# Layer 0's attention: values and row sums stored by DMA into turned tiles, and divided at the end

## The reference

```
h = layernorm(x) * (1 + ca) + sa
q, k, v = h @ W_query[n], h @ W_key[n], h @ W_val[n]        # per head n, width 8
att = softmax(q @ k.T * 8 ** -0.5)                          # 2048 x 2048 per head
x = x + ga * sum over n of (att @ v) @ W_out[n]
```

## Time and profile before

| what | us |
|---|---|
| median of 3 executions | 1732.26 |
| lowest and highest | 1729.99 and 1733.25 |
| span of the profiled execution | 1727.5 |
| VectorE busy in the span | 1303.3 (75%) |
| TensorE busy in the span | 1241.6 (72%) |
| ScalarE busy in the span | 890.0 (52%) |

### The profile page before, as it was taken

The page is one execution under the profiler, slowest core; times in us unless marked ns, Lnnn a source line. Parts: engine busy times, 40 slices in busy tenths (PEclk is TensorE's granted clock), DMA queues, the critical chain, the costliest instruction groups (busy, mean ns, idle before and its releaser), DMA issues. The chain is left out here.

```text
span 1727.5 us, 29793 instructions
## 1 busy us (share of the span) xinstructions
PE 1241.6 (72%) x10670; PEld 618.5 (36%) x10674; DVE 1303.3 (75%) x3511; ACT 890.0 (52%) x1757; POOL 235.6 (14%) x275
## 2 busy tenths in 40 slices
PE   7799999999999997575994463060315989823676
PEld 4122222222222223354983342040104556623445
DVE  5999999999999971447237336989898469668783
ACT  4099999999999997312421122020001675612463
POOL 2000000000000000003410314030001321100223
PEclk9599999999999999677995586575656898965668
DMA  2100000001000000000004331000001721022001
GB/s 69 41 10 27 25 20 21 21 26 27 27 21 20 21 3 1 15 30 1 1 1 183 102 86 47 0 0 1 1 1 26 208 70 47 18 101 63 22 22 31
DMA packets 45031, 62.88 MB, mean 36 GB/s; under 512 B 12785, under 2 KB 34357, under 8 KB 44485
## 3 DMA queue, kind: packets, MB, share of 16 engines
q1 hardware_dynamic: 38243, 49.71, 9.7%
q0 software_dynamic: 5440, 10.67, 2.5%
q10 hardware_dynamic: 1200, 0.59, 0.1%
HBM read 34.10 MB, written 13.63 MB: 28 GB/s over the span
## 5 line engine op out<-in xcount | busy, mean ns | idle before, releaser
L842 ACT ACTIVATE l0att_probs<-l0att_ps_sv 128x512 f32<-128x512 f32 x960 | 521.2, 596 | 79.7 <-PE l0att_ps_sv L811 67.9
L888 DVE TENSOR_REDUCE l0att_half_negmax<-l0att_ps_m 128x1 f32<-128x1024 f32 x480 | 547.0, 1215 | 5.3 <-PE l0att_ps_m L741 5.3
L773 PE MATMUL l0att_ps_sv<-l0att_probs,l_V_aug 128*32 128x256 f32 x4096 | 325.3, 392 | 4.8 <-ACT l0att_pv_sb L833 4.7
L811 PE MATMUL l0att_ps_sv<-l_Q,l_K 51*128 51x512 bf16 x992 | 194.4, 388 | 4.0 <-ACT l0att_probs L850 2.4
L741 PE MATMUL l0att_ps_m<-l_K,l_Q 48*128 48x512 bf16 x960 | 185.9, 384 | 11.1 <-DVE l0att_half_negmax L888 7.1
L773 PEld LDWEIGHTS l0att_ps_sv<-l0att_probs,l_V_aug 128*32 128x32 f32 x4096 | 83.0, 108 | 197.1 <-issue 100.5
L811 PEld LDWEIGHTS l0att_ps_sv<-l_Q,l_K 51*128 51x128 bf16 x992 | 48.0, 92 | 207.4 <-ACT l0att_probs L842 188.1
L472 POOL CAST l0att_nm<-l0att_negmax 128x16 bf16<-128x16 f32 x16 | 3.1, 196 | 514.5 <-DVE l0att_negmax L864 514.5
L2862 ACT ACTIVATE l3loc_probs<-l3loc_ps_s 128x320 f32<-128x320 f32 x128 | 48.9, 435 | 36.0 <-PE l3loc_ps_s L2839 35.4
L2040 DVE SCALAR_TENSOR_TENSOR l2spk_lif_v<-l2spk_U 128x64 f32<-128x64 f32 (+1 forms) x368 | 61.6, 211 | 0.0
L2305 PE MATMUL l2spk_ps<-l_X,l2spk_w_terms 128*128 128x512 bf16 x48 | 13.2, 445 | 62.3 <-DVE l_X L2335 62.3
(11 more groups left out here) (736 smaller groups left out, 2392.5 us busy)
## 6 DMA issues: line engine op xcount, KB each, us to landing
l_K<-l_kp SPq DMA_DIRECT2D x192, 32.0 KB
l_Q<-l_qp SPq DMA_DIRECT2D x192, 32.0 KB
l1ffn_W<-in_l_expert_w_dram SPq DMA_DIRECT2D x1, 4096.0 KB
l3f_experts_l_w<-in_l_w_dram SPq DMA_DIRECT2D x2, 2048.0 KB
l_sorted_in<-l1ffn_zeros SPq DMA_DIRECT2D x1, 3072.0 KB
l1exp_rows<-l_sorted_in SPq DMA_DIRECT2D x6, 512.0 KB, 5.6
l_sorted_out<-l1exp_y SPq DMA_DIRECT2D x6, 512.0 KB, 4.6
l_Q<-in_local_mask_q_dram POOLq DMA_DIRECT2D x2, 1170.0 KB, 18.8
```

The source lines that it names most:

```text
L773: mm = pe.matmul(ps_v[32 * c:32 * c + 32, cols], V_aug[:, kt, h, :], probs[:, kt % 2, c, cols], start=(kt == 0 and part == 0), stop=(kt == ...
L811: pe.matmul(dst, K[at, h % HEAD_BUFS, c1(kt)], Q[at, h % HEAD_BUFS, c4(2 * pair + i)], start=True, stop=True).then_inc(last_scored[i] if l ...
L842: act.activation(probs[:, kt % 2, c, :], ps_s[:, n % 3, :], ACT.Exp).then_inc(expd, 1)
L888: dve.tensor_reduce(half_negmax[:, h % 2, t, half:half + 1], src, AX_X, ALU.max, negate=True).then_inc(m_read, 1)
```

## The change

The turned form of the values is not left any more. `V_aug` gets 8 columns of ones instead of one, so `ps_v` holds the row sum 8 times, in rows 8 to 15 of each block. After ScalarE's copy, 8 transfers a head (4 blocks, values and sums) put the rows of `pv_sb` into `OT` and `den`, both [128, 2048] with head and value along the partitions. For heads 0 to 14 SP issues them; for head 15 SP, ScalarE and POOL share them. Heads 0 to 11 are divided in one piece on VectorE during the last head (`DIVIDED` = 96 rows), where the reciprocals of heads 12 to 14 are taken too. For head 15, the reciprocal is taken of the copied tile, and that is stored. The last 32 rows are multiplied in the output stage, one block of 512 tokens at a time. The turns of values on TensorE, the `"pv"` turns, the per-head reciprocal and multiplication, and the turning and copying of the output stage are gone. ScalarE's copy into a `pv_sb` buffer waits for the stores of the head two before it. `stage_project_out` stays for layer 3.

```diff
                 pool.wait_ge(norm.tile_normed, NT)
-                pool.memset(V_aug[:, :, :, L0_K + 1:], 0.0).then_inc(v_filled, 1)
-                pool.memset(V_aug[:, :, :, L0_K:L0_K + 1], 1.0).then_inc(v_filled, 1)
+                pool.memset(V_aug[:, :, :, L0_K + sums:], 0.0).then_inc(v_filled, 1)
+                pool.memset(V_aug[:, :, :, L0_K:L0_K + sums], 1.0).then_inc(v_filled, 1)
...
-def stage_l0_attend(nc, loads, g, V_aug, qp, kp, Q, K, ones_placed, loaded_first, O):
+STORES = 2 * NC4
+DIVIDED = 96
+def store_last(eng, OT, den, last_sb, copied, c, which, stored):
+    eng.wait_ge(copied[which], (L0_H, 1)[which])
+    store_rows(eng, OT, den, last_sb[which], L0_H - 1, c, which, stored)
+def store_rows(eng, OT, den, pv, h, c, which, stored):
+    rows = slice(L0_K * h, L0_K * (h + 1))
+    eng.dma_start((OT, den)[which][rows, c4(c)],
+                  pv[32 * c + L0_K * which:32 * c + L0_K * (which + 1), :]).then_inc(stored, 16)
+def stage_l0_attend(nc, loads, g, V_aug, qp, kp, Q, K, ones_placed, loaded_first, OT, den, heads_stored, last_stored):
...
         plan = {}
-        for s in range(-1, L0_H + 1):
-            slots = range(LEAD if s < 0 else NT if s < L0_H else 1)
+        for s in range(-1, L0_H):
+            slots = range(LEAD if s < 0 else NT)
...
                 uses = []
-                if s >= L0_H - 1 and kt == 3 * (L0_H - s):
-                    uses.append(("pv", s - 1))
...
                     place[what] = len(turns)
-                    if what[0] == "nm" and what[1] >= 2:
-                        place["pv", what[1] - 2] = len(turns)
...
             def _(sp):
+                def store_head(sp, h):
+                    sp.wait_ge(pv_copied, h + 1)
+                    for c in range(NC4):
+                        for which in range(2):
+                            store_rows(sp, OT, den, pv_sb[:, h % 2, :], h, c, which, heads_stored[h % 2])
...
                         load_piece(sp, Q, K, qp, kp, h, loaded[h % HEAD_BUFS], *piece)
+                    if h >= HEAD_BUFS:
+                        store_head(sp, h - HEAD_BUFS)
+                for h in range(L0_H - HEAD_BUFS, L0_H - 1):
+                    store_head(sp, h)
+                for c, which in ((0, 0), (0, 1), (3, 0)):
+                    store_last(sp, OT, den, last_sb, (pv_copied, rsum_done), c, which, last_stored[c])
...
                     splits_of(link, pool, [nm[:, h % 2, i, :] for i in range(3)], rest[:], negmax[:], nm_ready)
-                    if h >= 2:
-                        pool.wait_ge(nm_copied, h - 1)
-                    else:
-                        pool.wait_ge(m_read, place["nm", h] + 1)
+                    pool.wait_ge(m_read, place["nm", h] + 1)
...
                                        nm_rows[:, h % 2, :]).then_inc(nm_placed[h % 2], 16)
+                for which in range(2):
+                    store_last(pool, OT, den, last_sb, (pv_copied, rsum_done), 2, which, last_stored[2])
...
                             "p s t -> p (s t)"), ident16[:])
-                        if h >= 2:
-                            mm = turn_values(h - 2, dst)
-                    else:
-                        mm = turn_values(what[1], dst)
                     mm.then_inc(m_filled, 1)
-                def turn_values(h, dst):
-                    pe.wait_ge(pv_copied, h + 1)
-                    for i in range(4):
-                        mm = pe.transpose(dst[:, c1(i)], pv_sb[:, h % 2, c1(i)], g.ident[:])
-                    return mm
...
                     values(L0_H - 1, NT - 1, part)
-                run(("pv", L0_H - 1))
...
                     if h >= 2:
-                        act.wait_ge(m_filled, filled_by[place["pv", h - 2]])
+                        act.wait_ge(heads_stored[h % 2], 16 * STORES * (h // 2))
...
                 copy_values(L0_H - 1)
+                for c, which in ((1, 0), (1, 1), (3, 1)):
+                    store_last(act, OT, den, last_sb, (pv_copied, rsum_done), c, which, last_stored[c])
...
                                       ALU.min).then_inc(negmax_ready, 1)
-                def normalise(h, src):
-                    v = src[:, 0:BANK].rearrange("p (i c k) -> p i c k", i=4, c=NC4)
-                    if h >= 1:
-                        dve.wait_ge(m_read, place["pv", h - 1] + 1)
-                    link(dve.reciprocal(rden[:], v[:, :, :, L0_K]))
-                    o = O[:, :, L0_K * h:L0_K * (h + 1)].rearrange("p (c i) k -> p i c k", c=NC4)
-                    dve.tensor_tensor(o, v[:, :, :, 0:L0_K], bcast(rden[:].unsqueeze(3), P, 4, NC4, L0_K),
-                                      ALU.mult).then_inc(m_read, 1)
...
                         dve.tensor_copy(nm_rows[:, h % 2, :], src[0:3 * NT, BANK:BANK + P // 2].bitcast(BF16))\
-                           .then_inc(nm_copied if h >= 2 else m_read, 1)
-                        if h >= 2:
-                            normalise(h - 2, src)
-                    else:
-                        normalise(h, src)
+                           .then_inc(m_read, 1)
+                for parity in range(2):
+                    dve.wait_ge(heads_stored[parity], 16 * STORES * (DIVIDED // L0_K // 2))
+                early = slice(0, DIVIDED)
+                link(dve.reciprocal(den[early, :], den[early, :]))
+                dve.tensor_tensor(OT[early, :], OT[early, :], den[early, :], ALU.mult).then_inc(early_divided, 1)
+                dve.wait_ge(heads_stored[0], 16 * STORES * (L0_H // 2))
+                dve.wait_ge(heads_stored[1], 16 * STORES * (L0_H // 2 - 1))
+                late = slice(DIVIDED, P - L0_K)
+                dve.reciprocal(den[late, :], den[late, :]).then_inc(early_divided, 1)
+                dve.wait_ge(pv_copied, L0_H)
+                dve.reciprocal(rsum_sb[:], last_sb[0]).then_inc(rsum_done, 1)
+                dve.wait_ge(early_divided, 2)
...
+def stage_l0_out(nc, loads, w_name, g, name, OT, den, last_stored, gate_row):
+    with Stage(nc, name) as st:
+        w = loads[w_name]
+        ps_o = st.ps("ps_o", [P, 4, BANK])
+        w_gated = st.sem("w_gated")
+        divided = [st.sem(f"divided{c}") for c in range(NC4)]
+        summed = st.sem("summed")
+        chain = st.sem("chain")
+        def divide(eng, c):
+            eng.wait_ge(last_stored[c], 2 * 16)
+            left = OT[DIVIDED:P, c4(c)]
+            eng.tensor_tensor(left, left, den[DIVIDED:P, c4(c)], ALU.mult).then_inc(divided[c], 1)
+        with st.block() as block:
+            @block.tensor
+            def _(pe):
+                pe.wait_ge(w_gated, 1)
+                for t in range(NT):
+                    if t % 4 == 0:
+                        pe.wait_ge(divided[t // 4], 1)
+                    mm = pe.matmul(ps_o[:, t // 4, c1(t % 4)], OT[:, c1(t)], w[:], start=True, stop=True)
+                    if t % 4 == 3:
+                        mm.then_inc(summed, 1)
+            @block.vector
+            def _(dve):
+                dve.wait_ge(loads.done, loads.all)
+                dve.tensor_tensor(w[:], w[:], gate_row, ALU.mult).then_inc(w_gated, 1)
+                for c in range(2):
+                    divide(dve, c)
+                link = Chain(dve, chain)
+                for j in range(NC4):
+                    dve.wait_ge(summed, j + 1)
+                    xs = g.x[:, 4 * j:4 * j + 4, :]
+                    link(dve.tensor_tensor(xs, ps_o[:, j, :].rearrange("p (t f) -> p t f", t=4), xs, ALU.add))
+                    if j + 2 < NC4:
+                        divide(dve, j + 2)
+                    tile_stats(dve, g, g.x, range(4 * j, 4 * j + 4))
```

More of the change, by code:

```diff
@@ L483, in stage_project_parts @@
 def stage_project_parts(nc, loads, w_name, g, layer, name, V_aug, qp, kp, q=None, drams=(), stored=None, beside=None,
-                        rows_of_part=None):
+                        rows_of_part=None, sums=1):
     CHUNKS = 2 * NC4
@@ L637, in stage_l0_attend @@
         pv_sb = st.sb("pv_sb", [P, 2, BANK])
-        rden = st.sb("rden", [P, 4, NC4])
+        rsum_sb = st.sb("rsum_sb", [P, BANK])
+        last_sb = (pv_sb[:, (L0_H - 1) % 2, :], rsum_sb)
         ident16 = loads["ident16"]
@@ L652, in stage_l0_attend @@
         pv_done = st.sem("pv_done")
+        early_divided = st.sem("early_divided")
+        rsum_done = st.sem("rsum_done")
         pv_copied = st.sem("pv_copied")
@@ L656, in stage_l0_attend @@
         nm_ready = st.sem("nm_ready")
-        nm_copied = st.sem("nm_copied")
         nm_placed = [st.sem("nm_placed0"), st.sem("nm_placed1")]
@@ L958, in layer0_attention @@
             nc.sync.dma_start(K[at:at + 3], d["ones_l0"]).then_inc(ones_placed, 16)
-        O = st.sb("O", [P, NT, P])
+        OT = st.sb("OT", [P, S])
+        den = st.sb("den", [P, S])
+        heads_stored = [st.sem("even_heads_stored"), st.sem("odd_heads_stored")]
+        last_stored = [st.sem(f"last_stored{c}") for c in range(NC4)]
         V_aug = st.sb("V_aug", [P, NT, L0_H, 32])
@@ L967, in first_rows @@
```

(8 more changed lines are left out.)

## The result

The changed kernel takes 1736.58 us, the median of 20 runs (1732.72 to 1739.99), beside 1733.32 for the kernel before on the same chip (20 runs, 1729.86 to 1737.77). The ratio is 1.002, with a 95% interval of 1.0011 to 1.0029: slower by 3.3 us. The interval leaves out a ratio of 1, so the kernel is slower, but by how much is only known to lie between 1.9 and 5.0 us. The forecast was 1736.3.

The account below looks back on a forecast made before the run. VectorE and TensorE were both near full, the loop waiting on TensorE's next max product. Loop 0, tail +5.08 and last head -1.04 gave +4.0 on 1732.26: 1736.3 us, range 1732.0 to 1739.0.

Parts of the forecast that it names:

- The loop, gain 0: Heads 2 to 15: removing 14 reciprocals, 14 multiplications and 56 turns gains 0, heads staying at 37.33 us.
- The step that rested on head 1 of the kernel before: Head 1, lacking reciprocal, multiplication and turns, takes 37.33 us like a later head with them; so the loop gains 0.
- The rival of a loop that gains: Rival (7%): without the turns the next max product is ready earlier, up to 0.48 us a head, net -2.7, 1729.6.
- The last head, -1.04: From last negmax to last copy of values: two idles of 0.56 and 0.48 behind turns go, 1.04 us earlier.
- The stores of heads 0 to 14, 0: Eight transfers a head join SP's queue, about 19 of 37 us with the loads; a spare head covers them, cost nothing.
- The rival of a disturbed loop: Rival (5%): stores delay the negmax rows by 0.8 us in every head, 12 us in all, 1748.
- The reciprocals: 6.25 ns a column: two of 2048 columns at 12.95 us, hidden with 7 to spare; last of 512, 3.35, exposed.
- The fast and the dear reciprocal: Rivals: wide reciprocals stream, last costs 0.70, +1.4 us, 1733.6 (11%); or 8.3 ns a column, +5.7, 1738.0 (9%).
- Store, 2.10 plus a handover: Last head's sums: 2.10 us from store issue to landing, plus about 0.05 handover, before the first division of 0.70.
- 16.42: Sum in us from start of last copy to last statistics, where the kernel before takes 11.34: 5.08 longer.
- First product to first add, 2.03, and on to the statistics, 7.49: Output stage: first add 2.03 us after the products start, low clock adding 0.93; then 7.49 to last statistics.
- The sum: Tail 5.08 us longer, less 1.04 from the last head: +4.0 us; this forecast case had 68%.

Follow-up runs that it names:

- ladder: Changed kernel plus dummy reciprocals of 16 to 256 columns behind the copied negmax in heads 2 to 13; 1738.14 us, kernel before 1728.92 (1 run each).
- Warm: Changed kernel plus 21 and 5 idle TensorE products, behind the last values and ahead of the output products; 1738.49 us (5 runs), ratio to before 1.0041.
- direct: Changed kernel with the last head turned and divided 16 columns wide, no DMA, no engine meeting; 1731.57 and 1729.79 us, ratios to before 1.0002 and 0.999.
- short reciprocal: Changed kernel with the last reciprocal over 16 columns instead of 512, other columns undivided; 1733.99 us, kernel before 1728.92 (1 run each).
- shift: Kernel before plus idle memset and reciprocal of 640 columns ahead of gating layer 0's output weights; 1741.51 us (1 run), kernel before 1730.32 (23 runs).

## Why the prediction was right, point by point

*The loop, gain 0.* Right: 37.33 us a head before and after, idle of 0.39 in place of the divisions, and a room of 0.75 us that ladder measured. The step that rested on head 1 of the kernel before held. The groups on the pages say the same in sums: VectorE waits 10.9 us for the max products in all, where it waited 5.3. The rival of a loop that gains is out.

*The last head, -1.04.* Right: 39.87 instead of 40.87 us from the last negmax to the last copy, 1.00. The two negmax rows of VectorE's timelines, before and changed; the copies start at 677.49 and 674.20.

```profile
636.62 0.17 DVE L864 TENSOR_TENSOR l0att_negmax<-l0att_half_negmax 128x16 f32<-128x16 f32 x1
```

```profile
634.33 0.18 DVE L879 TENSOR_TENSOR l0att_negmax<-l0att_half_negmax 128x16 f32<-128x16 f32 x1
```

*The stores of heads 0 to 14, 0.* Right: heads didn't change, and ScalarE has no wait for a store in front of its copies of values. The rival of a disturbed loop is out.

*The reciprocals.* Right: the slope of 6.25 ns a column, read between widths of 8 and 16, held to 2048: 12.94 and 12.95 us against 12.95, and 3.35 against 3.35. They ended 8.5 us before they would have been in the way, where 7 were forecast. The fast and the dear reciprocal are both out. The latter is what the Trainium skill, page "VectorE: DVE Perf Modes", section "First, the fixed hardware budget", would have given with its repeat count of 8. Read as 8 cycles a column that is an estimated 8.3 ns, and no row here reaches it.

*Store, 2.10 plus a handover.* This is the step that was off. The transfer's size was right, but it is not what the division waited for. From the end of the reciprocal (678.18) to the first division (681.05) it took 2.87 us instead of 2.15. The prediction had summed what SP and ScalarE issue to 1.9 us, "just inside the 2.1", so it let the landing decide. But ScalarE's two issues took 1.40 instead of 1.2, which puts the last at 679.62, and the engines' meeting took until 680.73, 1.1 us instead of 0.4. Then the gate, 0.29. When the transfer landed can be read from the times at which the packed trace saw its semaphore raised: for the sums of the first 512 columns the last is 680.37, 2.16 us after the issue at 678.21 (2.16 in the other two traces too), and 0.68 us before the division. So the other path decided, the issues and the meeting, and it makes 0.7 of the 0.89 us by which the tail exceeds 16.42.

*First product to first add, 2.03, and on to the statistics, 7.49.* Right: 2.08 and 7.54. Warm took the clock's part, forecast as 0.93, out: its first add comes 1.14 us after the first product, 0.94 sooner.

*The sum.* Layer 0's attention and output came out at +5.97 - 1.00 = +4.97 us where +4.0 was forecast. The timed medians say +3.3 and, on another chip, +6.2, with intervals of 1.9 to 5.0 and 2.8 to 6.9 us. +5 lies at the edge of the first and inside the second, and +4 in both.

*Luck.* That 1736.3 met 1736.58 within 0.3 us is chance. The base of three runs, 1732.26, was 1.1 below the median of 20; layer 0's +4.0 was 1.0 too small; and the medians then differ by 1.7 less than layer 0 does. The mechanism was right, and the tail missed by 0.9; the rest cancelled.

*What the prediction left out.* It took what follows layer 0's attention as untouched. In the traces it is not: 1044.6 against 1038.7 us, which with +4.97 and an attention that began 2.3 us earlier makes up the 8.6 between the spans. How much of that lies in the medians can be estimated by taking each kernel's layer 0 difference from its timed one. For changed that is 3.3 - 5.0 = -1.7 and 6.2 - 5.0 = +1.2; for direct, whose layer 0 is 1.5 us shorter than before's, 0.7 + 1.5 = +2.2 and -0.5 + 1.5 = +1.0; for warm 8.17 - 4.04 = +4.1, from 5 runs. So it lies between -1.7 and +4.1 us, of either sign for the changed kernel, with an uncertainty of 1.5 to 4 us each from the ratios' intervals. That is enough to hide warm's 0.93 us, which is plain in the tail; that it did so was not shown.

One part of what the traces lose is in layer 0's feed-forward part: from its first norm to layer 1's it takes 70.6 us in the first and third traces of the changed kernel, 65.6 in the second, and 66.9 and 68.1 before, so it does not go with the change. The other part is layer 3's attention, which is longer in all ten other traces than in the two of before. There the granted clock was at its lower level (0.50) for 57.5 and 58.3 us before and for 60.4 to 67.1 in the others. At half the rate the 6.6 us between 58.3 and 64.9 (third trace of the changed kernel) are worth an estimated 3.3, and layer 3's attention is 3.3 longer. Elsewhere the agreement is looser: in ladder the estimate is 1.0, and it is 2.2 longer. These lengths are from the record of the granted clock in the packed traces, between the two norms of the table.

For one such stretch the traces show what went ahead. First rows of TensorE's timeline, from the second trace of before and from the third of the changed kernel.

```profile
1500.27 0.45 PE L2839 MATMUL l3loc_ps_s<-l_Q,l_K 123*128 123x160 bf16 x4 [0.72 <-DMA l_Q<-l3loc_nm_rows]
```

```profile
1509.00 0.64 PE L2901 MATMUL l3loc_ps_s<-l_Q,l_K 123*128 123x160 bf16 x4 [2.00 <-DMA l_Q<-l3loc_nm_rows]
```

Then the windows around them, in the same order.

```profile
1501.00:1505.00 4.00, 4.00 (x92) 2.97 (x84) 1.45 (x4) 3.42 (x11) 0.00 (x0) 1.00 0.00 0
```

```profile
1506.90:1510.90 4.00, 2.00 (x36) 1.32 (x24) 0.49 (x1) 1.26 (x5) 0.00 (x0) 0.78 0.01 1
1510.90:1514.90 4.00, 4.00 (x74) 3.05 (x74) 0.74 (x3) 2.68 (x8) 0.00 (x0) 0.80 0.02 4
```

TensorE waits 2.00 us for a transfer where before it waited 0.72, and from 1509.1 on, as it starts again, the clock is low. The five traces with this low stretch (the three of the changed kernel, ladder, short reciprocal) all have a wait of 1.8 to 2.0 us at that transfer; the other seven have 0.7 or 0.8 and no low stretch there. Warm, direct and shift are longer by low stretches elsewhere in layer 3. What makes that transfer late for TensorE, and why no trace of the other programs is as short as before's two, stays open: shift makes the delay a candidate, no run isolates it, and with two traces of before it can be the scatter of executions or the place of the instructions as well.

## What to carry to other kernels

Work that leaves a busy engine is worth only what the engines next wait for: compare the loop with a head of the same trace that lacks the work, or put dummy work of growing size at that place, and the room is read off before anything is rewritten. Dividing 16 narrow columns on each of 128 partitions and dividing 512 wide ones is the same arithmetic laid out differently, and the reciprocal is paid by the column; where the wide form can hide, as for heads 0 to 14, it is free, and at the end of a chain it is 3.1 us longer, of which taking it out gave back 2.2. So change a layout for the iterations that have cover, and keep the short path for the last one. And ask whether the change can win at all: direct, which does just that, is 1.5 us shorter in layer 0 and in the timed whole only level with the kernel before, since the loop had nothing to give.

## What the runs showed of the hardware that was not expected

- VectorE's reciprocal has one straight line from 8 to 2048 columns, within 0.02 us: 0.203 us, 0.253 (16, and 0.23 in ladder), 0.64 (80), 0.94 (128), 1.33 (192), 1.73 (256), 3.35 (512), 4.15 (640), 12.94 (2048). 24 partitions take as long as 96.
- ScalarE's first store of the tail took 1.46 us to issue, and two that followed 1.40 together. SP took 0.62 for a store where its loads took 0.563, GpSimd 0.57 and 0.53.
- The meeting of the engines between the two stages took 1.1 us after the last issue of a store in the changed kernel and 0.87 in short reciprocal. Without stores ahead of it, VectorE waited 0.39 us for it before and 0.56 in shift.
- The store of the first 512 columns of sums raised its semaphore for the last time 2.16 us after SP began to issue it, in each of three traces.
- TensorE's granted clock fell to 0.50 behind a wait of 1.8 to 2.0 us for a transfer in layer 3, in five traces of five, and not behind one of 0.7 to 0.8 at the same place, in seven of seven.
- A delay of 4.6 us in layer 0, in a kernel otherwise unchanged, came with a longer rest of the span, by 5.4 and 8.7 us against the two traces of before. Of a gain below 1 us made early in this kernel, the timed whole showed nothing.
